# Rope queries relayed through memory by half batch, head and dimension: one store and four loads for a chunk instead of one and sixteen

## The chip, the cores and the metric

The kernel runs on one core of a Trainium2 chip. The metric is the device time of one execution in microseconds (us), the median of several runs. The core has four engines that compute (TensorE, VectorE, ScalarE and GpSimd; in the profile PE, DVE, ACT and POOL), 16 DMA engines that move data between memory (HBM) and on-chip memory (SBUF), and SyncE (SP), which here does nothing but wait for semaphores and issue DMAs, one after the other.

## The reference, cut to what matters

One decoder layer over 16 sequences of 128 tokens with 1024 features: latent attention with 32 heads, a cross attention, and a feed-forward part. The change touches the position-dependent half of the attention's scores:

```
q_rope = (c_q @ w_q_up_rope).reshape(b, s, H, DR).transpose(0, 2, 1, 3)      # H = 32 heads, DR = 64
q_rope = _apply_rope(q_rope, inv_freq, mscale)
scores = einsum('bhsr,btr->bhst', q_lat, c_kv) + einsum('bhsd,btd->bhst', q_rope, k_rope)
probs = softmax(where(causal, scores / sqrt(DN + DR), min))
```

After the attention come `x = x + out @ w_out`, then the cross attention and the feed-forward part, which the change leaves as they are.

## The kernel before

Everything is written out by hand: each engine has its own instruction list, and semaphores order them. The attention works through 16 passes ("quads" in the code, `m` from 0 to 15): two groups of 8 sequences, and for each group 8 quads of four heads. A pass has 8 steps (`s`), four for each of its two chunks (`c`) of 512 tokens, which are 4 sequences. Passes 0 to 6 are of the kind "full" (beside the attention they prepare the weights of the next quad), pass 7 is "switch" (tokens of the second group are loaded), passes 8 to 14 are "later" and 15 is "last", beside which the cross attention starts.

The rope queries of a chunk are computed for four heads at once. VectorE and GpSimd leave them in `rope_tmp`, `[128, 4, 512]`: the partition is head times 32 plus dimension, and the four slots are the first and the second half of the dimensions, each as a high and a low part, whose sum is the value. For the scores TensorE wants the four parts of one head pair on the partitions, in `qrope[c]`. Partitions can't be exchanged on chip in one step, so the data makes a round through memory: `relayout_out` stores `rope_tmp` to `parts_d[c]`, and `relayout_in` waits until that has landed and loads it back in the other order. There are 32 such rounds (16 passes, 2 chunks), of 1 MB each way. Both stand in SyncE's list, in front of whatever is issued next:

- in a full pass (`full_quad`) chunk 1's loads stand ahead of `load_raw_rope`, which brings the next quad's rope weights; ScalarE cuts them into high and low parts (L1924) in the middle of the same pass. Chunk 1's store stands ahead of a load of raw head weights (`load_head`, L678), which ScalarE reads at L1797 and L1798. Chunk 0's store and loads stand ahead of another `load_head`.
- in the switch pass (`switch_quad`) chunk 0's round stands ahead of `store_x1`, and chunk 1's ahead of `load_wqr(1)`, which brings the rope weights that TensorE needs in pass 8 (L55 on `at_wqr`).
- in pass 14 (`later_quad`) chunk 1's round stands ahead of `load_wvo` and, behind that, of the first rows `cr_x` of the cross attention (`load_x1`, L976), which VectorE reads in pass 15 at L2851, between two steps of the attention.
- at the start (`preparation`) chunk 0's round is on the way to the first scores (L1276).

DMAs issued by SyncE go through one queue and share the 16 DMA engines; TensorE waits for `qrope_in[c]` before the first step of each chunk.

Of the kernel before, what the change touches and what calls it, by code (L numbers as in the profile page):

```python
# [16 lines left out]
P = 128  # L17
# [5 lines left out]
HALF = DR // 2  # L23
# [24 lines left out]
def as_f32(ap):  # L48

    return ap.bitcast(F32)  # L50
# [9 lines left out]
def decoder(nc, a, scratch, out_d):  # L60
# [124 lines left out]
    with ctx:  # L185
# [22 lines left out]
        compressed = [home(4 * (PACK * c + KEYS), f"at_keys{c}", [P, CH]) for c in range(CPG)]  # L208
        wabs = [home(49152 + 6144 * i, f"at_wabs{i}", [P, 2, WABS_W], F32R) for i in range(2)]
        wqr = home(61440, "at_wqr", [P, 2, WQR_W], F32R)  # L210
        qrope0 = home(67584, "at_qrope0", [P, 2, HALVES, PAIR, HQ], F32R)
        qlat1 = home(83968, "at_qlat1", [P, HALVES, PAIR, HQ])
        rope_tmp = home(92160, "at_rope_tmp", [P, 4, CH])
        qlat0 = home(100352, "at_qlat0", [P, HALVES, PAIR, HQ])
# [17 lines left out]
        stage_at = (4 * (PACK + UNUSED), 4 * UNUSED, 198656)  # L232
        stage_0, stage_1, stage_2 = (home(o, f"at_stage{i}", [P, CH]) for i, o in enumerate(stage_at))
        stage = [[stage_0, stage_1], [stage_0, stage_2]]
        qrope1 = home(174080, "at_qrope1", [P, 2, HALVES, PAIR, HQ], F32R)
        ring = [home(200928 + 4 * ITEM_B * i, f"ab_raw{i}", [P, ITEM_B]) for i in range(2)]

        uv_hi = home(83456, "ab_uv_hi", [P, DV], F32R)
# [433 lines left out]
        def _(sp):  # L672
# [15 lines left out]

            def relayout_out(m, c):
                sp.wait_ge(rope_lo, 2 * (ROPES * m + c + 1))  # L690
                sp.dma_start(parts_d[c], rope_tmp[:]).then_inc(parts_out[c], 16)

            def relayout_in(m, c):
                sp.wait_ge(parts_out[c], 16 * (m + 1))
                of = parts_d[c].rearrange("(h p) j n -> j p h n", h=QUAD)
                for j in range(4):
                    for h in range(QUAD):
                        to = as_f32(qrope[c][j * HALF:(j + 1) * HALF, h // PAIR, :, h % PAIR])
                        sp.dma_start(to, of[SLOT_OF_PART[j]][:, h].rearrange("p (k q) -> p k q", q=HQ)).then_inc(  # L699
                            qrope_in[c], 16)  # L700

            def load_tokens(c, lo, hi, done):
                sp.dma_start(as_f32(tok[:, c, lo:hi]), tok_d[c][:, lo:hi]).then_inc(done[c], 16)
# [66 lines left out]
            def preparation():  # L770
                load_w_down(0)
                sp.dma_start(xt[:, 0, :], x_turned[ORDER[0]][:, 0, :]).then_inc(x_first_in, 16)
                load_w_down(1)
                sp.dma_start(xt[:, 1, :], x_turned[ORDER[0]][:, 1, :]).then_inc(xt_in[0], 16)
                load_w_down(2)
                load_turned(0, 1)
                load_w_down(3)
                load_w_down(4)
                load_turned(0, 2)
                load_x_tile(0, 0)  # L780
                load_w_down(5)
                load_x_tile(0, 1)
                load_turned(0, 3)
                load_x_tile(0, 2)
                sp.dma_start(ident[:], consts["ident"]).then_inc(ident_in, 16)
                load_x_tile(0, 3)
                load_w_turned(0)
                load_turned(1, 0)
                load_w_turned(1)
                load_turned(1, 1)  # L790
                for to, name in ((mask, "mask"), (cos, "cos"), (sin, "sin")):
                    sp.dma_start(to[:], consts[name]).then_inc(const_in, 16)
                for p in range(2):
                    sp.sem_inc(wabs_out[p], 16)
                    sp.sem_inc(wvo_out[p], 16 * len(RUNS[0]))
                sp.sem_inc(wqr_out, 16)

                def store_queries(i):
                    sp.wait_ge(tok_lo, 4 * i + QT)
                    sp.dma_start(tok_d[i][:, 0:KEYS], as_f32(tok[:, i, 0:KEYS])).then_inc(cq_out[i], 16)  # L800

                def store_keys(i):
                    sp.wait_ge(zeroed, 1)
                    sp.wait_ge(kr_lo, i + 1)
                    sp.wait_ge(tok_lo, 4 * i + 4)
                    sp.wait_ge(prep_turn_taken, lo_at["kv", i] + 1)
                    sp.dma_start(tok_d[i][:, KEYS:UNUSED], compressed[i][:]).then_inc(key_out[i], 16)
                    sp.dma_start(tok_d[i][:, KV_HI:PACK], as_f32(tok[:, i, KV_HI:PACK])).then_inc(key_out[i], 16)

                load_x_tile(1, 0)  # L810
                load_pair(0, 0, 0)
                load_x_tile(1, 1)
                load_pair(0, 1, 1)
                load_turned(1, 2)
                load_x_tile(1, 2)
                load_x_tile(1, 3)
                load_turned(1, 3)
                load_turned(2, 0)
                store_queries(0)
                load_turned(2, 1)  # L820
                for t in range(2):
                    load_x_tile(2, t)
                load_turned(2, 2)
                load_x_tile(2, 2)
                store_keys(0)
                load_x_tile(2, 3)
                sp.wait_ge(ab_mm, 2)
                load_head(0, 0, 0)
                store_wabs(0, 0, 2)
                load_turned(2, 3)  # L830
                sp.wait_ge(ab_mm, 4)
                load_head(0, 1, 1)
                store_wabs(0, 1, 4)
                load_turned(3, 0)
                store_queries(1)
                load_turned(3, 1)
                load_turned(3, 2)
                store_keys(1)


                sp.wait_ge(cq_out[1], 16)
                sp.wait_ge(key_out[1], 2 * 16)
                for t in range(BPC):
                    load_x_tile(3, t)
                load_raw_rope(0)
                sp.wait_ge(ab_mm, 6)
                load_head(0, 2, 0)
                load_turned(3, 3)
                sp.wait_ge(ab_mm, 8)
                load_head(0, 3, 1)  # L850
                store_wqr(0)
                relayout(0, 0)

                sp.wait_ge(qrope_in[0], 256)
                sp.wait_ge(prep_turn_taken, lo_at["x", KT * N - 1] + 1)
                load_x(0, 0)
                relayout_out(0, 1)
# [266 lines left out]
        def _(pe):  # L1124
# [136 lines left out]
            def score_ropes(m, s, group):  # L1261

                pair, c = place(s)
                if not (isinstance(m, int) and STEPS * m + s == 0):
                    pe.wait_ge(score_taken, STEPS * m + s)
                if s % UNITS == 0:
                    if group:
                        pe.wait_ge(key_in[c], 2 * 16)
                    pe.wait_ge(qrope_in[c], 256 * (m + s // STEPS + 1))
                if s == UNITS and not group:  # L1270

                    pe.wait_ge(kr_lo, N)
                    pe.wait_ge(tok_lo, 4 * N)
                rope_keys = tok[:, c, KR_HI:KR_HI + 2 * CH].rearrange("p (part t) -> p part t", part=2)
                for bl in range(2):
                    pe.matmul(score[:, bl], both_heads(qrope[c][:, pair, half_of(s, bl, 1)]), rope_keys[:, :, batch_cols(s, bl)],  # L1276
                              start=bl == 0, stop=False, skip_group_check=True)
                for bl in range(2):
                    pe.matmul(score[:, EARLY, :, early_keys(bl)], both_heads(qrope[c][:, pair, half_of(s, bl, 0)]),
                              rope_keys[:, :, early_cols(s, bl)], start=bl == 0, stop=False, skip_group_check=True)  # L1280

            def score_rests(m, s, taken):
# [1166 lines left out]
        def _(dve):  # L2449
# [287 lines left out]
            def opening():  # L2737
                first = USES_PREPARED
                largest(0, 0)
                dve.memset(as_f32(pT_both[HQ:P, :, :, 0:HQ]), 0.0)  # L2740
                query(N - 1, 1)
                query(N - 1, 2)
                recip(0, 0)

                latent(0, 1, 0, first + 4)
                latent(0, 1, 1, first + 5)
                largest(0, 1)
                turn(0, 0)
                dve.wait_ge(parts_out[0], 16)
                rope_keys(N - 1, (1,))  # L2750
                rope_half(0, 1, 0, first + 6)
                recip(0, 1)
                rope_half(0, 1, 1, first + 7)
                rope_keys(N - 1, (0,))
                direct_values(0, 0)
                value_sums(0, 0)
                kv_values(N - 1)

                dve.wait_ge(val_lo_done, 1)
                dve.wait_ge(prep_turn_taken, lo_at["kv", N - 1] + 1)  # L2760
                dve.sem_inc(added, 2)
                keys(N - 1)
# [367 lines left out]
def build(nc, a, out):  # L3130

    def scratch(name, shape):
# [1 line left out]

    decoder(nc, a, (scratch("tok_d", [CPG, P, PACK]), scratch("wabs_d", [QUADS, P, 2, 2 * PAIR * QL]),
                    scratch("wvo_d", [QUADS, P, 2, 2 * 7 * CH]), scratch("wqr_d", [QUADS, P, 2 * QT * 2 * P]),
                    scratch("parts_d", [CPG, P, 4, CH]), scratch("x1_d", [TOKENS // GROUPS, D]),
                    scratch("x2_d", [TOKENS, D]), scratch("ff_w_d", [7 * 3, P, 4 * CH])), out)


# [68 lines left out]
```

## Time and profile before

| | |
|---|---|
| median of 3 runs | 1919.39 us (1919.37 to 1921.03) |
| the profiled execution | 1921.1 us, of it 1919.3 us from the first to the last instruction (the span) |
| TensorE busy | 1899.9 us, 99% of the span |
| VectorE, ScalarE, GpSimd busy | 1546.6, 1183.9, 1039.1 us |
| mean clock granted to TensorE | 0.998 of full speed |
| DMA queue of SyncE | 207232 packets, 392.24 MB, 58.7% of the 16 engines' span |
| packets under 512 bytes | 146688 |

The span is what the instructions cover; the profiled execution is 1.8 us longer, for what lies before and after it. Busy shares are means over stages with different limits. A packet is what one DMA engine moves as one unbroken run.

### The profile page before, as it was taken

What the parts mean: (1) busy time and instruction counts of PE and PEld (TensorE: products, weight loads), DVE (VectorE), ACT (ScalarE), POOL (GpSimd) and SP (SyncE); (2) the same over time, 40 slices, a digit from 0 to 9 for tenths busy, and PEclk for the clock granted to TensorE, in tenths of its full rate; (3) what the DMA queues carried; (4) which work ended last, traced back from release to release, by engine and by line L of the source; (5) the groups of instructions that cost most, each with busy time, mean ns of one, the idle gap of its engine ahead of it and who ended that gap; (6) DMA issues with size and microseconds to landing.
All of it is one profiled execution on the core that took longest, in us unless ns stands there. A gap on an engine that the chain in (4) does not pass through costs nothing.

```text
span 1919.3 us, 32626 instructions
## 1 busy us (share of the span) xinstructions
PE 1899.9 (99%) x9920; PEld 1600.2 (83%) x9920; DVE 1546.6 (81%) x3168; ACT 1183.9 (62%) x2904; POOL 1039.1 (54%) x1019
## 2 busy tenths in 40 slices
PE   9999999999999999999999999999999999999999
PEld 7888888888888888888888888888887878888887
DVE  6778888887888888887888787887877889996677
ACT  5457767676758575765655556655655658766441
POOL 5468778787869696964655556555664511000000
PEclk9999999999999999999999999999999999999999
DMA  9838464646465655587646364464637287466644
GB/s 356 332 109 305 148 257 126 252 131 247 141 238 163 230 172 197 200 300 286 219 165 200 112 230 131 159 186 156 229 90 286 82 288 256 193 223 238 236 151 175
DMA packets 207323, 393.30 MB, mean 205 GB/s; under 512 B 146688, under 2 KB 147456, under 8 KB 188160
## 3 DMA queue, kind: packets, MB, share of 16 engines
q1 hardware_dynamic: 207232, 392.24, 58.7%
q8 instruction: 39, 0.64, 0.1%
q14 instruction: 52, 0.43, 0.1%
HBM read 236.46 MB, written 155.71 MB: 204 GB/s over the span
## 4 chain that ended last, share of the span: by engine, by line
PE 87%; DMA 5%; SPq 4%; DVE 2%; issue 1%; POOL 1%; ACT 0%; DVEq 0%; ACTq 0%; POOLq 0%
PE at_out L1325 9%; PE at_out L1329 9%; PE at_out L1326 9%; PE at_qbank L55 7%; PE at_qbank L57 7%; PE at_qbank L56 7%; SPq L699 3%; PE at_qbank L1649 3%; PE at_score L1649 3%; PE at_score L1286 2%; PE at_out L1649 2%; DMA parts_d<-at_rope_tmp 2%; PE at_score L1289 2%; PE at_turned L1300 2%; PE at_value L55 2%; PE at_value L56 2%
## 5 line engine op out<-in xcount | busy, mean ns | idle before, releaser
L2684 DVE TENSOR_TENSOR at_acc<-at_out,at_acc 128x512 f32<-128x512 f32 x640 | 438.8, 689 | 133.1 <-PE at_out L1329 127.0
L2315 POOL TENSOR_TENSOR at_acc<-at_stage,at_acc 128x512 f32<-128x512 f32 x256 | 331.7, 1296 | 175.6 <-ACT at_stage L1791 165.9
L1325 PE MATMUL at_out<-at_wvo,at_val_hi 128*128 128x512 f32 x896 | 365.5, 408 | 3.9 <-DVE at_acc L2684 3.0
L1329 PE MATMUL at_out<-at_wvo,at_val_lo 128*128 128x512 f32 x896 | 351.8, 393 | 0.0
L1326 PE MATMUL at_out<-at_wvo,at_val_hi 128*128 128x512 f32 x896 | 350.3, 391 | 0.0
L1791 ACT ACTIVATE at_stage<-at_out 128x512 f32<-128x512 f32 x256 | 152.4, 599 | 91.8 <-PE at_out L1329 80.1
L1329 PEld LDWEIGHTS at_out<-at_wvo,at_val_lo 128*128 128x128 f32 x896 | 168.4, 188 | 38.8
L1325 PEld LDWEIGHTS at_out<-at_wvo,at_val_hi 128*128 128x128 f32 x896 | 168.8, 188 | 32.9 <-DVE at_acc L2684 6.1
L1832 ACT ACTIVATE at_pT<-at_turned 128x256 fp32r<-128x256 f32 x128 | 48.9, 382 | 234.9 <-PE at_turned L1300 234.9
L1326 PEld LDWEIGHTS at_out<-at_wvo,at_val_hi 128*128 128x128 f32 x896 | 169.2, 189 | 26.1
L1827 ACT ACTIVATE at_probs<-at_probs,at_row_stats 128x128 f32<-128x128 f32 (+1 forms) x512 | 184.0, 361 | 8.4 <-DVE at_row_stats L2631 8.4
L2301 POOL TENSOR_TENSOR at_val_lo<-at_val_whole,at_val_hi 128x512 fp32r<-128x512 f32 x128 | 165.2, 1290 | 9.0 <-ACT at_val_hi L1845 8.3
L2274 POOL TENSOR_TENSOR at_probs<-at_probs,at_row_stats 128x256 f32<-128x256 f32 x128 | 78.7, 615 | 155.7 <-DVE at_row_stats L2636 155.2
L55 PE MATMUL at_qbank<-at_tok,at_wabs 128*128 128x512 f32 x384 | 153.1, 399 | 2.0 <-DVEq L2581 2.0
L57 PE MATMUL at_qbank<-at_tok,at_wabs 128*128 128x512 f32 x384 | 150.6, 392 | 0.0
L56 PE MATMUL at_qbank<-at_tok,at_wabs 128*128 128x512 f32 x384 | 149.3, 389 | 0.0
L2282 POOL TENSOR_TENSOR at_rope_tmp<-at_rope_tmp 128x512 f32<-128x512 f32 x62 | 79.0, 1295 | 81.1 <-DVE at_rope_tmp L2590 81.1
L2643 DVE TENSOR_TENSOR at_pT<-at_turned,at_pT 64x128 fp32r<-64x128 f32 x256 | 73.6, 288 | 48.6 <-ACT at_pT L1834 43.4
L1845 ACT ACTIVATE at_val_hi<-at_val_whole 128x512 fp32r<-128x512 f32 x128 | 80.7, 630 | 45.8 <-DVE at_val_whole L2664 45.7
L1812 ACT ACTIVATE at_qlat<-at_qbank 128x512 f32<-128x512 f32 x128 | 75.7, 591 | 47.3 <-PE at_qbank L57 47.3
L1827 ACT ACTIVATION_READ_ACCUMULATOR at_probs<-at_probs,at_row_stats 128x1 f32 x512 | 95.8, 187 | 0.0
L55 PEld LDWEIGHTS at_qbank<-at_tok,at_wabs 128*128 128x128 f32 x384 | 72.0, 187 | 23.7 <-DVEq L2581 8.2
(323 smaller groups left out, 5047.1 us busy)
## 6 DMA issues: line engine op xcount, KB each, us to landing
parts_d<-at_rope_tmp SPq DMA_DIRECT2D x32, 1024.0 KB, 6.5
at_qrope<-parts_d SPq DMA_DIRECT2D x512, 64.0 KB, 2.1
wvo_d<-at_wvo SPq DMA_DIRECT2D x16, 2048.0 KB, 8.2
at_wvo<-wvo_d SPq DMA_DIRECT2D x16, 2048.0 KB, 7.4
ff_w_d<-ff_w SPq DMA_DIRECT2D x21, 1024.0 KB, 6.3
ff_w<-ff_w_d SPq DMA_DIRECT2D x21, 1024.0 KB, 4.8
ab_raw<-in_w_heads SPq DMA_DIRECT2D x32, 576.0 KB, 5.0
wvo_d<-at_wvo SPq DMA_DIRECT2D x16, 1024.0 KB, 9.9
```

Source lines behind the costliest of these rows:

```text
L55: pe.matmul(out, w_hi, x_hi, start=first, stop=False)
L56: pe.matmul(out, w_hi, x_lo, start=False, stop=False)
L57: return pe.matmul(out, w_lo, x_hi, start=False, stop=last)
L1325: pe.matmul(out, hi, weight[:, 0], start=start, stop=False, skip_group_check=True)
L1326: pe.matmul(out, hi, weight[:, 1], start=False, stop=False, skip_group_check=True)
L1329: pe.matmul(out, lo, weight[:, 0], start=False, stop=True, skip_group_check=True).then_inc(out_ready, 1)
L1649: ins = pe.matmul(out, ff_w[i][:, k, cols], x[:, k, :], start=first, stop=last, skip_group_check=True)
L1791: act.activation(stage[group][z][:], outb[FACTORS[name][2]][:], ACT.Copy).then_inc(staged, 1)
L1827: ins = act.activation(rows, rows, ACT.Exp, bias=nmax[i][:, j:j + 1], accum_out=sums[i][:, j:j + 1])
L2301: pool.tensor_tensor(val_lo[s % 2][:, SUMS], val_whole[s % 2][:, SUMS], as_f32(val_hi[s % 2][:, high(SUMS)]), ALU.subtract).then_inc(val_s ...
L2315: pool.tensor_tensor(at, stage[group][z][:], at, ALU.add).then_inc(pool_added, 1)
L2684: dve.tensor_tensor(at, outb[FACTORS[name][2]][:], at, ALU.add).then_inc(added, 1)
```

## The change

The store writes `parts_d[c]` as `[32, 128, 64]`: first the slot and the half batch (4 slots times 8 halves of 64 tokens), then head and dimension, then the 64 tokens. Each unbroken run in memory is then 64 numbers, 256 bytes, where it was 2048 numbers, 8 KB. In that order the load of one slot is a single DMA over 32 partitions, with 32 runs of 256 bytes for each; there are four loads where there were sixteen (one for each slot and head). `qrope` has its dimensions in another order, `[half, head, token]` instead of `[head pair, half, head of the pair, token]`; the 128 numbers that TensorE loads at once lie together in both. The waits on `qrope_in` count to 64 instead of 256. Apart from that one `memset` of VectorE's opening is placed three instructions later.

```
-        qrope0 = home(67584, "at_qrope0", [P, 2, HALVES, PAIR, HQ], F32R)
+        qrope0 = home(67584, "at_qrope0", [P, HALVES, QUAD, HQ], F32R)
...
             def relayout_out(m, c):
                 sp.wait_ge(rope_lo, 2 * (ROPES * m + c + 1))
-                sp.dma_start(parts_d[c], rope_tmp[:]).then_inc(parts_out[c], 16)
+                sp.dma_start(parts_d[c].rearrange("n p q -> p n q"),
+                             rope_tmp[:].rearrange("p j (k q) -> p (j k) q", q=HQ)).then_inc(parts_out[c], 16)
 
             def relayout_in(m, c):
                 sp.wait_ge(parts_out[c], 16 * (m + 1))
-                of = parts_d[c].rearrange("(h p) j n -> j p h n", h=QUAD)
+                of = parts_d[c].rearrange("(j k) (h p) q -> j p (k h) q", j=4, h=QUAD)
                 for j in range(4):
-                    for h in range(QUAD):
-                        to = as_f32(qrope[c][j * HALF:(j + 1) * HALF, h // PAIR, :, h % PAIR])
-                        sp.dma_start(to, of[SLOT_OF_PART[j]][:, h].rearrange("p (k q) -> p k q", q=HQ)).then_inc(
-                            qrope_in[c], 16)
+                    to = as_f32(qrope[c][j * HALF:(j + 1) * HALF]).rearrange("p k h q -> p (k h) q")
+                    sp.dma_start(to, of[SLOT_OF_PART[j]]).then_inc(qrope_in[c], 16)
...
-                sp.wait_ge(qrope_in[0], 256)
+                sp.wait_ge(qrope_in[0], 64)
...
-                    pe.wait_ge(qrope_in[c], 256 * (m + s // STEPS + 1))
+                    pe.wait_ge(qrope_in[c], 64 * (m + s // STEPS + 1))
...
-                    pe.matmul(score[:, bl], both_heads(qrope[c][:, pair, half_of(s, bl, 1)]), rope_keys[:, :, batch_cols(s, bl)],
+                    pe.matmul(score[:, bl], both_heads(qrope[c][:, half_of(s, bl, 1), heads]), rope_keys[:, :, batch_cols(s, bl)],
...
-                dve.memset(as_f32(pT_both[HQ:P, :, :, 0:HQ]), 0.0)
                 query(N - 1, 1)
                 query(N - 1, 2)
                 recip(0, 0)
+                dve.memset(as_f32(pT_both[HQ:P, :, :, 0:HQ]), 0.0)
...
-                    scratch("parts_d", [CPG, P, 4, CH]), scratch("x1_d", [TOKENS // GROUPS, D]),
+                    scratch("parts_d", [CPG, 4 * CH // (SEQ // 2), P, SEQ // 2]), scratch("x1_d", [TOKENS // GROUPS, D]),
```

From the change on, line numbers above 694 are one lower.

The order of instructions changes on SyncE alone, apart from the memset. This is the start of a full pass in SyncE's list, the loads of chunk 1 (`at_qrope_92`) between a load of raw weights and `load_raw_rope`, before:

```order
L674 DMA ab_raw_93<-in_w_heads 128x2x512
L694 REGISTER_ALU
L699 DMA at_qrope_92<-parts_d 32x8x64 x16
L681 ISA
L681 DMA at_rope_tmp<-in_w_rope 128x768
```

And with the change:

```order
L674 DMA ab_raw_93<-in_w_heads 128x2x512
L695 REGISTER_ALU
L699 DMA at_qrope_92<-parts_d 32x32x64 x4
L681 ISA
L681 DMA at_rope_tmp<-in_w_rope 128x768
```

Twelve DMAs fewer stand ahead of the raw rope weights; the neighbours are the same.

The second place is the switch pass, from chunk 0's store to the load of the rope weights of pass 8 (`at_wqr`), in SyncE's list before:

```order
L691 DMA parts_d<-at_rope_tmp 128x2048
L699 DMA at_qrope_61<-parts_d 32x8x64 x16
L716 DMA x_d<-at_acc 128x4x1024
L706 DMA at_keys_57<-tok_d 128x512
...
L713 DMA at_acc<-in_x 128x2x1024
L691 DMA parts_d<-at_rope_tmp 128x2048
L699 DMA at_qrope_92<-parts_d 32x8x64 x16
L747 DMA at_wqr<-wqr_d 128x1536
L743 DMA at_wvo_68<-wvo_d 128x4096
```

And with the change:

```order
L691 DMA parts_d<-at_rope_tmp 128x32x64
L699 DMA at_qrope_61<-parts_d 32x32x64 x4
L715 DMA x_d<-at_acc 128x4x1024
L705 DMA at_keys_57<-tok_d 128x512
...
L712 DMA at_acc<-in_x 128x2x1024
L691 DMA parts_d<-at_rope_tmp 128x32x64
L699 DMA at_qrope_92<-parts_d 32x32x64 x4
L746 DMA at_wqr<-wqr_d 128x1536
L742 DMA at_wvo_68<-wvo_d 128x4096
```

Nothing changes places; each store has 32 runs of 64 numbers for each partition instead of one of 2048, and 12 loads fewer follow it.

## Rows read from the trace of the kernel before

**Rows 1.** The page: busy us of each engine (share of the span) xinstructions

```profile
PE 1899.9 (99%) x9920; PEld 1600.2 (83%) x9920; DVE 1546.6 (81%) x3168; ACT 1183.9 (62%) x2904; POOL 1039.1 (54%) x1019
```

**Rows 2.** Waits of PE, 150 to 720 us: us in total, times, longest

```profile
PE at_value L55 <- DVE at_pT L2643: 4.0, 6, 1.0
```

**Rows 3.** Timeline, SyncE, a full pass: start us, us, issue, count

```profile
236.11 7.95 SPq L699 DMA_DIRECT2D at_qrope<-parts_d  x16
```

**Rows 4.** Timeline, ACT and PE, the same pass: [idle before <-releaser]

```profile
247.76 0.85 ACT L1924 ACTIVATE at_wqr<-at_rope_tmp 128x768 fp32r<-128x768 f32 x1 [1.07 <-DMA at_rope_tmp<-in_w_rope]
250.15 0.38 PE L55 MATMUL at_value<-at_pT,at_tok 128*128 128x256 f32 x1 [1.05 <-DVE at_pT L2643]
```

**Rows 5.** Timeline, SyncE, the switch pass

```profile
842.31 9.24 SPq L699 DMA_DIRECT2D at_qrope<-parts_d  x16
...
861.80 0.47 SPq L691 DMA_DIRECT2D parts_d<-at_rope_tmp  x1
880.55 9.30 SPq L699 DMA_DIRECT2D at_qrope<-parts_d  x16
889.89 0.45 SPq L747 DMA_DIRECT2D at_wqr<-wqr_d  x1
```

**Rows 6.** Timeline, PE, start of pass 8

```profile
894.58 0.79 PE L55 MATMUL at_qbank<-at_tok,at_wqr 128*128 128x512 f32 x1 [2.91 <-DMA at_wqr<-wqr_d]
```

**Rows 7.** Windows: us, busy of each engine, PEclk (granted clock), DMA share, GB/s

```profile
250.20:253.60 3.40, 3.10 (x15) 2.39 (x16) 3.14 (x7) 2.64 (x6) 2.84 (x3) 1.00 1.01 432
894.30:897.70 3.40, 3.12 (x7) 2.48 (x8) 0.00 (x0) 0.00 (x0) 0.00 (x0) 0.50 1.00 429
1474.60:1478.00 3.40, 3.40 (x13) 2.90 (x12) 2.12 (x4) 0.15 (x1) 1.97 (x3) 0.50 1.02 419
```

**Rows 8.** Timeline, SyncE, from pass 14 into pass 15

```profile
1450.61 7.73 SPq L699 DMA_DIRECT2D at_qrope<-parts_d  x16
1458.60 1.42 SPq L743 DMA_DIRECT2D at_wvo<-wvo_d  x3
1460.36 1.01 SPq L976 DMA_DIRECT2D cr_x<-x_d  x2
```

**Rows 9.** Timeline, DVE and PE, pass 15

```profile
1471.47 0.69 DVE L2851 BATCH_NORM_STATS2 cr_stats<-cr_x 128x6 f32<-128x512 f32 x1 [2.87 <-DMA cr_x<-x_d]
1474.26 0.54 PE L1325 MATMUL at_out<-at_wvo,at_val_hi 128*128 128x512 f32 x1 [3.05 <-DVE at_acc L2684]
```

**Rows 10.** DMA queues, 331.2 to 333 us: packets, MB, share of 16 engines

```profile
q1 hardware_dynamic: 1562, 0.44, 110.4%
```

**Rows 11.** The same of 113.5 to 117.3 us

```profile
q1 hardware_dynamic: 144, 1.05, 66.1%
```

**Rows 12.** The same of 1916.5 to 1918.6 us

```profile
q1 hardware_dynamic: 303, 0.27, 37.0%
```

**Rows 13.** The page, DMA issues: count, KB each, median us to landing

```profile
at_qrope<-parts_d SPq DMA_DIRECT2D x512, 64.0 KB, 2.1
```

**Rows 14.** Timeline of SyncE and ACT just behind chunk 1's store, full pass

```profile
320.47 0.34 SPq L678 DMA_DIRECT2D ab_raw<-in_w_heads  x1
...
329.60 0.30 ACT L1797 ACTIVATE ab_uv_hi<-ab_raw 128x128 fp32r<-128x128 f32 x1
```

**Rows 15.** DMA issues, 319.8 to 320.6 us: KB each, us to landing

```profile
ab_raw<-in_w_heads SPq DMA_DIRECT2D x1, 576.0 KB, 5.5
```

**Rows 16.** Timeline, SyncE and PE, the first round

```profile
117.32 7.98 SPq L699 DMA_DIRECT2D at_qrope<-parts_d  x16
126.88 0.40 SPq L709 DMA_DIRECT2D at_acc<-in_x  x1
...
127.82 0.40 PE L1276 MATMUL at_score<-at_tok,at_qrope 128*128 128x256 f32 x2
```

**Rows 17.** Timeline, DVE, the opening

```profile
131.54 0.48 DVE L2740 MEMSET at_pT<- 64x512 f32 x1 [0.16 <-issue]
...
134.78 0.43 DVE L2620 TENSOR_TENSOR at_probs<-at_score,at_mask 128x256 f32<-128x256 f32 x1 [1.36 <-PE at_score L1289]
```

More of the change, by code:

```diff
@@ L234, in decoder @@
         stage = [[stage_0, stage_1], [stage_0, stage_2]]
-        qrope1 = home(174080, "at_qrope1", [P, 2, HALVES, PAIR, HQ], F32R)
+        qrope1 = home(174080, "at_qrope1", [P, HALVES, QUAD, HQ], F32R)
         ring = [home(200928 + 4 * ITEM_B * i, f"ab_raw{i}", [P, ITEM_B]) for i in range(2)]
@@ L1273, in score_ropes @@
                     pe.wait_ge(tok_lo, 4 * N)
+                heads = slice(pair * PAIR, (pair + 1) * PAIR)
                 rope_keys = tok[:, c, KR_HI:KR_HI + 2 * CH].rearrange("p (part t) -> p part t", part=2)
                 for bl in range(2):
-                    pe.matmul(score[:, bl], both_heads(qrope[c][:, pair, half_of(s, bl, 1)]), rope_keys[:, :, batch_cols(s, bl)],
+                    pe.matmul(score[:, bl], both_heads(qrope[c][:, half_of(s, bl, 1), heads]), rope_keys[:, :, batch_cols(s, bl)],
                               start=bl == 0, stop=False, skip_group_check=True)
                 for bl in range(2):
-                    pe.matmul(score[:, EARLY, :, early_keys(bl)], both_heads(qrope[c][:, pair, half_of(s, bl, 0)]),
+                    pe.matmul(score[:, EARLY, :, early_keys(bl)], both_heads(qrope[c][:, half_of(s, bl, 0), heads]),
                               rope_keys[:, :, early_cols(s, bl)], start=bl == 0, stop=False, skip_group_check=True)
```

## Prediction

> **What bounds the kernel now.** I read the page first: TensorE is busy for 1899.9 of 1919.3 us [rows 1]. A change that takes nothing from TensorE can win only part of the 19.4 us left, so the question is which of TensorE's gaps a round of rope queries stands behind. I then took its waits (who released it), looked at the timeline just before each, and followed the releaser back. None of the waits names `qrope` itself, but three kinds go back to SyncE's list, where the round keeps something else from being issued.
>
> First, the full passes. TensorE waits six times for the transposed probabilities, 4.0 us in all [rows 2]. In the pass shown it idles 1.05 us at 250.15; ScalarE, which turns the probabilities ahead of that, had itself idled 1.07 us for the raw rope weights [rows 4]. These are issued right behind sixteen loads, which took SyncE 7.95 us from 236.11 on, and landed at 247.76 [rows 3, 4].
>
> Second, the switch pass. TensorE idles 2.91 us for `at_wqr` until 894.58 [rows 6]. That load was issued at 889.89, behind 9.30 us of sixteen loads, which began when the store issued at 861.80 had landed, at 880.55 [rows 5]. Right behind the stall the granted clock is 0.50 (1.2 GHz, the lower level) for 3.40 us or so [rows 7]; work done in that time at half speed costs 1.7 us more.
>
> Third, pass 15. VectorE idles 2.87 us for `cr_x` until 1471.47, and TensorE then 3.05 us for VectorE [rows 9]. `cr_x` was issued at 1460.36 behind 3.5 MB of `at_wvo`, issued at 1458.60, and that behind 7.73 us of sixteen loads [rows 8]. Again the clock is 0.50 for 3.40 us [rows 7], 1.7 us more. Behind the 1.05 us stall in the full pass it stays 1.00, 2.4 GHz [rows 7].
>
> So 4.0 + (2.91 + 1.7) + (3.05 + 1.7) = 13.4 us is the most that the change can win.
>
> **The price of small packets.** Each load has always moved packets of 256 bytes: 4096 for a round. In a stretch with the queue full of them the 16 engines were 110.4% busy with 1562 packets in 1.8 us [rows 10]: by time, 1.8 x 16 / 1562 = 18.4 ns each. A round's loads are 256 packets for each DMA engine, 4.7 us; now they take 7.7 to 9.3 us because SyncE issues sixteen. Four issues don't bound them (one takes 0.5 us, from 7.73 / 16), so I take 2.1 us from issue to landing for 64 KB [rows 13], less its own 0.3 us of packets (16 x 18.4 ns), plus 4.7: 6.5 us from the first issue to the last landing. Now it is 126.88 - 117.32 = 9.6 us in the first round [rows 16].
>
> The store is the disputed cost. Today its 1 MB runs in 8 KB packets: 66.1% of 3.8 us x 16 engines for the megabyte [rows 11], 2.5 us of a full queue. With the change it is 256 packets for each engine too. No row shows 256-byte packets written to memory. From below it can't be less than today's 2.5 us. The nearest row with small packets into memory is the output's end, mostly 1 KB packets: 37.0% of 2.1 us x 16 over 303 packets is 41 ns each [rows 12]; 1 KB at the pace of the 8 KB packets would be 39 ns, so a write carries no visible extra. From above I take twice the 18.4 ns. I use 18.4 ns, as the loads show: 4.7 us, 2.2 us more than now for each of the 32 stores.
>
> A rule of the Trainium skill speaks against this: the page "DMA: Bandwidth & Descriptors", section Specifications, asks for at least 512 B for line rate, below which the DMA engine does a read-modify-write. For the loads' 256 bytes the trace shows no more than 18.4 ns, 223 GB/s; for writes to memory nothing here shows it. By that rule, if it doubled the write, the sum would be that of the first rival below, where it is worked out from rows.
>
> **The sum.**
> - Full passes: the loads start at 236.11 as before and have landed by 242.6 (6.5 us), some 1 us later where a raw-weight load is ahead. The raw rope weights, 0.4 MB right behind them, land about 3 us earlier than 247.76; ScalarE was free at 246.69 (247.76 - 1.07). The wait goes, six times: -4.0.
> - Switch pass: chunk 0's last load is issued 0.5 us before 842.31 + 9.24 and lands 2.1 later, 853.2. With the change the store lands 2.2 later and the loads 6.5 after: 851.0, 2.2 earlier. From there to 880.55 the queue is full of what stands behind (the store issued at 861.80 needs 18.7 us), so chunk 1's store lands 2.2 earlier and 2.2 later: 880.55 again. Four loads (1.8 + 4.7) and 768 KB at 0.4 MB/us (rows 7 has 429 GB/s), 1.9 us: `at_wqr` is there at 889.0; TensorE wants it at 891.67. The wait and its dip go: -4.6. Margin 2.7 us.
> - Pass 15: the store lands at 1452.8, the loads at 1459.3 instead of about 1460.0 (1458.34, less 0.5, plus 2.1). `at_wvo` is issued in time and starts right behind them, about 0.8 us earlier than now, and so does `cr_x`. TensorE's stall falls from 3.05 to 2.2. Whether the clock then stays up is open: it does after 1.05 us and not after 2.91. I take it that it does: -0.8 - 1.7 = -2.5.
> - First round: landed at 117.32 + 2.2 + 6.5 = 126.0 instead of 126.9, and TensorE wants it at 127.82 [rows 16]: 0.
> - Raw head weights behind chunk 1's store: now issued at 320.47, landed 5.5 later at 326.0, read at 329.60 [rows 14, 15]. 3.6 us of cover, of which 2.2 go: 0.
> - The memset: 0.48 us, moved into VectorE's 1.36 us of idle time before 134.78 [rows 17]: 0. Without that cover it would be 0.5 us.
> - TensorE's own work: the same matmuls on 128 neighbouring numbers, 0.
>
> Together -11.1 us. The profiled execution took 1921.1 us, 1.7 above the median of the runs; against the median, **1919.4 - 11.1 = 1908.3 us**.
>
> **Rivals.**
>
> *The stores are slow (slower).* One mechanism: a 256-byte packet into memory takes much longer than 18.4 ns. It decides at about 26 ns. At twice, 36.8 ns, a store is 9.4 us, 6.9 more than now. The raw head weights land 6.9 later against 3.6 of cover, ScalarE waits 3.3 us in each of seven passes, at most 23.1 us; the first scores wait 2.9 + 1.7; `at_wqr` lands 3.8 later than now; pass 15 loses 4.0; the 4.0 of the full passes are still won: +31.5, 1951 us. At 26 ns (4.15 more): +3.9, +0.2, -1.6, +1.3, -4.0, about 0: 1919. For it: nothing shows such writes. Against it: rows 12. Chance 0.16 for above, 0.07 for around 26 ns (no change), 0.10 for 21 to 25 ns (1911 to 1916).
>
> *Four big loads take as long as sixteen small ones (slower).* They read memory in runs of 256 bytes 8 KB apart, where they now read 2 KB together. If they take 7.7 us or more, nothing is won in full passes, `at_wqr` comes 4.4 later (two stores), pass 15 loses 2.2 and the first round 1.3: +7.9, 1927 us. It decides from 7 us of packets on. Against it: when the queue was full the engines kept their pace [rows 10]. Chance 0.05.
>
> *The clock dips in pass 15 all the same:* -9.4, 1910 us. *Or the whole stall there goes,* if the loads run a little faster: -13.4, 1906 us. Both belong to the forecast's own range, 1905.5 to 1911; chance of all this 0.57.
>
> **How the numbers follow.** What a measurement here can tell from no change is 0.2%, 3.8 us. Faster: 0.57 + 0.10 + 0.05 of other partial gains = 0.72. Same: 0.07. Slower: 0.16 + 0.05 = 0.21, the two slow rivals. The range runs from 1904.5 (all gains, a little more) into the slow cases, which lie between 1921 and 1951: at 1926 about 0.15 are left above.
>
> **What the profile would show.** Right: 1 MB stores landing some 2 us later than now where the queue is empty (4.7 to about 7), four issues in 2 to 5 us; no ScalarE wait at L1924 and no gap at L55 `at_value` in full passes; no stall around 890; one dip of the clock or none. Wrong: packets of the store above 26 ns, ScalarE idle at L1797, TensorE idle at L1276.

## The result, and the profile after

The changed kernel takes **1907.59 us** (median of 4 runs, 1906.41 to 1910.56), the kernel before 1919.76 (median of 4 runs beside them, 1919.37 to 1921.03). The ratio is 0.9942, 95% interval 0.9926 to 0.9957: 12.2 us less. The profiled execution took 1908.6 us, with a span of 1906.8. Forecast were 1908.3 and a range of 1904.5 to 1926.

The page of the changed kernel, busy time of each engine, the packets and the issues of the round:

```profile
PE 1895.3 (99%) x9920; PEld 1597.3 (84%) x9920; DVE 1545.4 (81%) x3168; ACT 1183.8 (62%) x2904; POOL 1039.5 (55%) x1019
...
DMA packets 328154, 393.27 MB, mean 206 GB/s; under 512 B 271616, under 2 KB 272384, under 8 KB 313088
...
parts_d<-at_rope_tmp SPq DMA_DIRECT2D x32, 1024.0 KB, 7.1
at_qrope<-parts_d SPq DMA_DIRECT2D x128, 256.0 KB, 4.6
```

TensorE's busy time fell by 4.6 us against [rows 1] with the same 9920 matmuls; two stretches of 3.4 us at half the clock [rows 7] that are gone make 3.3 of these by an estimate (half of the 3.12 and 3.40 us of work in them). The rest of the gain, 7.9 of the 12.5 us by which the span is shorter, is idle time. The longest of TensorE's waits from 150 to 720 us, in us in total, times and longest:

```profile
PE at_qbank L55 <- DVEq L2581: 2.0, 7, 0.3
```

The wait for `at_pT` of [rows 2] is no longer there. (The line numbers of the two kernels agree again at L1276 and up to L2740, since the change adds a line there too, `heads = slice(pair * PAIR, (pair + 1) * PAIR)`.) The timeline of SyncE in the changed kernel in the first round, in a full pass, in the switch pass and in pass 14, at the places of [rows 16, 3, 5, 8]:

```profile
113.14 0.38 SPq L691 DMA_DIRECT2D parts_d<-at_rope_tmp  x1
118.68 2.73 SPq L699 DMA_DIRECT2D at_qrope<-parts_d  x4
125.36 0.40 SPq L708 DMA_DIRECT2D at_acc<-in_x  x1
...
236.28 4.95 SPq L699 DMA_DIRECT2D at_qrope<-parts_d  x4
241.42 0.86 SPq L681 DMA_DIRECT2D at_rope_tmp<-in_w_rope  x1
...
854.48 0.47 SPq L691 DMA_DIRECT2D parts_d<-at_rope_tmp  x1
873.54 2.62 SPq L699 DMA_DIRECT2D at_qrope<-parts_d  x4
876.21 1.08 SPq L746 DMA_DIRECT2D at_wqr<-wqr_d  x1
...
1442.17 2.75 SPq L699 DMA_DIRECT2D at_qrope<-parts_d  x4
1445.19 1.93 SPq L742 DMA_DIRECT2D at_wvo<-wvo_d  x3
```

The first store of the kernel before:

```profile
112.82 0.33 SPq L691 DMA_DIRECT2D parts_d<-at_rope_tmp  x1
```

Three spans matter here. The first store takes 118.68 - 113.14 = 5.5 us until the loads can be issued, where it took 117.32 - 112.82 = 4.5 (its loads are in [rows 16]). The first round's loads take 125.36 - 118.68 = 6.7 us against 9.6 [rows 16]. And in the full pass the raw weights are issued 5.1 us behind the first load, where they stood behind 8 us of issues [rows 3]. What the other engines show, as timelines of ScalarE, VectorE and TensorE:

```profile
246.75 0.83 ACT L1924 ACTIVATE at_wqr<-at_rope_tmp 128x768 fp32r<-128x768 f32 x1
...
886.72 0.39 PE L55 MATMUL at_qbank<-at_tok,at_wqr 128*128 128x512 f32 x1
...
1461.26 0.69 DVE L2851 BATCH_NORM_STATS2 cr_stats<-cr_x 128x6 f32<-128x512 f32 x1 [2.20 <-DMA cr_x<-x_d]
...
1464.05 0.50 PE L1325 MATMUL at_out<-at_wvo,at_val_hi 128*128 128x512 f32 x1 [2.38 <-DVE at_acc L2684]
```

Neither L1924 nor `at_wqr` has a wait behind it now [rows 4, 6]; of the large stalls only that for `cr_x` is left, 2.38 us instead of 3.05 [rows 9]. The granted clock stays at 1.00 behind it (windows):

```profile
1464.10:1467.50 3.40, 3.40 (x22) 2.95 (x23) 2.92 (x6) 1.25 (x4) 2.23 (x3) 1.00 1.02 411
```

To place gains and losses, the table gives, for each profiled execution, the start of TensorE's first L1276 of a pass (the last row but one is the last of the 8 steps of pass 15): for before in us, for the others as the difference to it. e1 to e4 are the experiments below.

| | before | changed | e1 small store | e2 weights first | e3 big loads | e4 double store |
|---|---|---|---|---|---|---|
| pass 0 | 127.82 | +0.29 | +1.24 | +0.05 | +0.07 | +0.34 |
| pass 1 | 213.63 | +0.17 | +1.22 | +0.04 | -0.05 | +0.76 |
| pass 7 | 767.49 | -4.77 | +2.20 | -5.06 | -5.10 | -0.11 |
| pass 8 | 854.47 | -4.79 | +2.71 | -5.04 | -5.11 | +4.96 |
| pass 9 | 941.39 | -9.47 | +4.78 | -8.23 | -9.79 | +1.20 |
| pass 15 | 1435.37 | -9.54 | +9.16 | -7.67 | -9.88 | +8.57 |
| its last step | 1504.81 | -11.67 | +10.92 | -8.02 | -14.29 | +10.05 |
| end | 1919.31 | -12.48 | +11.22 | -8.48 | -14.44 | +10.04 |

So the full passes 1 to 6 gave 4.9 us, pass 8 (with the stall of [rows 6]) 4.7, pass 15 2.1, and the part behind it 0.8.

### The profile page after: what moved, and what is told of

Same layout as the page of the kernel before. It is cut to its first block, busy times and chain, and to the rows that moved or that the text cites. A ratio compares the mean times of both kernels' runs of the same rounds, so it can differ in the third digit from the quotient of the medians.

```text
span 1906.8 us, 32242 instructions
## 1 busy us (share of the span) xinstructions
PE 1895.3 (99%) x9920; PEld 1597.3 (84%) x9920; DVE 1545.4 (81%) x3168; ACT 1183.8 (62%) x2904; POOL 1039.5 (55%) x1019
## 4 chain that ended last, share of the span: by engine, by line
PE 89%; POOL 3%; DVE 2%; DMA 2%; issue 1%; SPq 1%; ACT 1%; DVEq 0%; POOLq 0%; ACTq 0%
PE at_out L1325 10%; PE at_out L1329 9%; PE at_out L1326 9%; PE at_qbank L55 7%; PE at_qbank L57 7%; PE at_qbank L56 7%; PE at_qbank L1649 3%; PE at_score L1649 3%; PE at_score L1286 3%; PE at_out L1649 2%; PE at_score L1289 2%; PE at_turned L1300 2%; PE at_value L55 2%; PE at_value L56 2%; PE at_value L57 2%; PE at_value L1649 2%
## 5 line engine op out<-in xcount | busy, mean ns | idle before, releaser
L55 PE MATMUL at_qbank<-at_tok,at_wabs 128*128 128x512 f32 x384 | 153.0, 398 | 2.0 <-DVEq L2581 2.0
L55 PEld LDWEIGHTS at_qbank<-at_tok,at_wabs 128*128 128x128 f32 x384 | 72.0, 187 | 23.6 <-DVEq L2581 8.1
```

Of the source, the lines that this page charges most:

```text
L55: pe.matmul(out, w_hi, x_hi, start=first, stop=False)
```

## The experiments

My theory: a round's loads used to keep other loads from being issued, and the gain is theirs; the small-packet store costs a little and hides. The rivals: the gain has to do with fewer issues as such, or the store's price is far from what I took, or the loads' time has another cause than their packets.

**The store with sixteen loads (e1).** The changed layout and store, with sixteen loads. These read the new layout, in runs of 256 bytes where they read 2 KB together, so that it isn't the store alone that differs from the kernel before:

```
-                sp.dma_start(parts_d[c], rope_tmp[:]).then_inc(parts_out[c], 16)
+                sp.dma_start(parts_d[c].rearrange("n p q -> p n q"),
+                             rope_tmp[:].rearrange("p j (k q) -> p (j k) q", q=HQ)).then_inc(parts_out[c], 16)
...
-                of = parts_d[c].rearrange("(h p) j n -> j p h n", h=QUAD)
+                of = parts_d[c].rearrange("(j k) (h p) q -> j h p k q", j=4, h=QUAD)
...
-                        sp.dma_start(to, of[SLOT_OF_PART[j]][:, h].rearrange("p (k q) -> p k q", q=HQ)).then_inc(
+                        sp.dma_start(to, of[SLOT_OF_PART[j]][h]).then_inc(
```

> The kernel before with the change's memory layout and its store in runs of 256 bytes, but still sixteen loads for a round. If the store costs what the first round of the changed kernel showed (5.5 us from issue to landing against 4.5 before, 1.0 more): the rope weights of pass 8 land 2.0 later (two stores), TensorE's wait for them grows from 2.9 to about 5; pass 15 loses 1.0, the first round 0.2; the raw head weights keep their cover: +3.3 us, 1923. If it costs the 2.2 us of the forecast: 4.4 in the switch pass, 2.2 in pass 15, 1.3 in the first round, +7.9 us, 1928. If, against both, writing in small runs were what gains time: below 1918.

Measured: 1930.63 us (5 runs), ratio 1.0055 (1.0042 to 1.0068), **slower** by 10.8 us, more than either theory gave (3.3 and 7.9). Timelines of SyncE and TensorE, and TensorE's waits from 940 to 1436 us:

```profile
113.18 0.38 SPq L691 DMA_DIRECT2D parts_d<-at_rope_tmp  x1
118.70 8.35 SPq L700 DMA_DIRECT2D at_qrope<-parts_d  x16
```
```profile
899.24 0.74 PE L55 MATMUL at_qbank<-at_tok,at_wqr 128*128 128x512 f32 x1 [4.79 <-DMA at_wqr<-wqr_d]
...
1484.07 0.79 PE L1326 MATMUL at_out<-at_wvo,at_val_hi 128*128 128x512 f32 x1 [3.70 <-DVE at_acc L2685]
```
```profile
PE at_qbank L55 <- DMA at_wqr<-wqr_d: 2.7, 6, 0.6
```

and its window behind the stall of 3.70 us:

```profile
1484.00:1491.00 7.00, 6.93 (x26) 6.17 (x27) 5.03 (x14) 1.55 (x6) 3.04 (x5) 0.58 1.04 408
```

The store costs 118.70 - 113.18 = 5.5 us again. The sixteen loads take about as long as before: from first issue to last landing the median of the rounds for passes 9 to 15 is 9.6 us, in the kernel before 9.4. So the reading in another order costs little, and most of the loss is the store's. `at_wqr` in pass 8 fits the price of 1 us (4.79 instead of 2.91, expected about 5). Three other places do not. The first scores begin 1.24 us later, where 0.2 was expected by this price. Passes 1 to 7 lose 1.5. Pass 15 loses 1.8 instead of 1.0: the stall is only 0.65 longer, but the clock is low for about 6 us behind it, where it was for 3.4 [rows 7]. What both theories lacked altogether is in the row before the window: two stores, 1 us later each, make TensorE wait for `at_wqr` in all six passes from 9 to 14. In the kernel before it landed there only 0.1 to 1.2 us before TensorE took it (in pass 10 at 1060.53, read at 1060.67). The table has 4.4 us for these passes, of which the wait names 2.7. So the store is not free: in front of sixteen loads it costs the kernel 11 us, and it is the four loads that turn this into a gain of 12.

**The order alone (e2).** The kernel before, old store and sixteen loads, two weight loads moved ahead of them:

```
-                relayout_in(q, 1)
                 if not (isinstance(q, int) and q == 0):
+                    sp.wait_ge(parts_out[1], 16 * (q + 1))
                     load_raw_rope(q + 1)
+                relayout_in(q, 1)
...
-                relayout(m + 1, 1)
+                relayout_out(m + 1, 1)
                 sp.wait_ge(rope_mm, 2 * ROPES * (m + 2))
                 load_wqr(1)
+                relayout_in(m + 1, 1)
```

> The kernel before, with the 8 KB store and the sixteen loads, but with two loads of weights moved ahead of the sixteen: the raw rope weights in full passes and at_wqr in the switch pass. If the gain of the change comes from what these loads waited behind: the full passes win 4 to 5 us, the switch pass 4.6 with its dip of the clock, pass 15 nothing: 1919.8 - 9 = 1910.5, and the wait for cr_x stays at about 2.9. If the gain comes from fewer issues or fewer descriptors as such, or if the queries are then late in their turn (sixteen loads behind 0.4 MB more): less than half of that, 1915 or more, with waits of TensorE at L1276.

Measured: 1912.11 us (5 runs), ratio 0.9955 (0.9942 to 0.9969), **faster** by 7.7. Timeline of SyncE in e2, the full pass and the switch pass, then TensorE:

```profile
236.28 0.34 SPq L681 DMA_DIRECT2D at_rope_tmp<-in_w_rope  x1
236.67 8.00 SPq L699 DMA_DIRECT2D at_qrope<-parts_d  x16
...
857.32 0.43 SPq L747 DMA_DIRECT2D at_wqr<-wqr_d  x1
876.20 8.42 SPq L699 DMA_DIRECT2D at_qrope<-parts_d  x16
```
```profile
897.75 0.49 PE L1327 MATMUL at_out<-at_wvo,at_val_hi 128*128 128x512 f32 x1 [0.89 <-DMA at_wvo<-wvo_d]
...
1466.09 0.50 PE L1327 MATMUL at_out<-at_wvo,at_val_hi 128*128 128x512 f32 x1 [2.55 <-DVE at_acc L2686]
```

With all sixteen loads still there the full passes win 5.1 us, as in the change (4.9), and neither shows the wait for `at_pT` of [rows 2]. So their gain needs neither fewer loads nor the new layout, only that the raw weights are issued earlier. The switch pass gives 3.2 instead of 4.7: `at_wvo`, still behind the sixteen loads, is now late by 0.89. Pass 15 stays at a stall of 2.55. The theory holds for two of the three places; in the third this run moved nothing.

**Large packets for the loads (e3).** The store does the whole rearrangement, one store for each head, and the loads read 8 KB in one piece:

```
+                for h in range(QUAD):
+                    sp.dma_start(parts_d[c][:, :, h],
+                                 rope_tmp[h * HALF:(h + 1) * HALF].rearrange("p j (k q) -> p (j k) q", q=HQ)).then_inc(
+                        parts_out[c], 16)
...
+                of = parts_d[c].rearrange("p (j k) h q -> j p (k h q)", j=4)
```

> The changed kernel with the rearrangement done by the store alone: four stores in runs of 256 bytes (one for each head), and four loads that read 8 KB in one piece. If small packets are what bounds a round's loads (6.7 us from first issue to last landing): they fall to about 4, four store issues cost about 1.2, and the wait for cr_x in pass 15 shrinks by 2 to 3 us: 1905.5. If four issues and their latency bound them, or the four stores take longer than one: nothing or a loss, 1907.5 to 1911.

Measured: 1906.83 us (5 runs), ratio 0.9933 (0.992 to 0.9946), which the intervals do not tell from the change's 0.9942. The time lies between those of the two theories, but the loads did not fall to the 4 us of the first. The page of e3:

```profile
DMA packets 202714, 393.28 MB, mean 206 GB/s; under 512 B 142080, under 2 KB 142848, under 8 KB 183552
...
at_qrope<-parts_d SPq DMA_DIRECT2D x128, 256.0 KB, 4.9
```

It moves 38% fewer packets, yet a load takes 4.9 us instead of 4.6. My account of the loads, 256 packets of 18.4 ns for each engine, gave the right 6.5 us for what looks like the wrong reason; e6 tests it the other way round. That pass 15 has no stall for `cr_x` in this execution (the table's -14.29) says little, as e5 and e10 will show: the same list without this edit had 2.38, 1.16 and none.

**What bounds a round's loads (e6, e9).** Both write the same megabyte with four loads that each fill all 128 partitions instead of 32. They leave the rearrangement out, so that the scores are computed from other numbers, and they also read memory in another order than the runs they stand beside. e6 keeps packets of 256 bytes:

```
-                of = parts_d[c].rearrange("(j k) (h p) q -> j p (k h) q", j=4, h=QUAD)
+                of = parts_d[c].rearrange("n p q -> p n q")
...
+                    some = slice(HALVES * j, HALVES * (j + 1))
+                    sp.dma_start(to[:, some], of[:, some]).then_inc(qrope_in[c], 16)
```

> The changed kernel with four loads of the same size, the same packets of 256 bytes and the same places in the list, but each writes to all 128 partitions (8 of the 32 runs of each) and not to 32; this leaves the rearrangement out, so the scores are of other numbers. If the loads are bound by writing to 32 partitions at a time (the 8 KB packets of the big loads took 6.8 us for a round too): a round's loads fall from 6.7 us to about 5.6, the 3.6 us of a full queue that a store of 256-byte packets takes plus 2, and the wait in pass 15 shrinks by about 1: 1906.5. If they are bound by the number of packets, as the forecast had it: 6.7 us as before, 1907.6.

e9 does it on e3, in runs of 2 KB (`some = slice(CH * j, CH * (j + 1))`).

> As the whole-width loads, with the same part left out, but by four loads of 2 KB runs (and the four stores by head, as with the big loads): 512 packets on all 128 partitions, where the big loads had 128 packets on 32 at a time. If the 32 partitions are the bound: some 4.5 us from first issue to last landing against 6.8 of the big loads. If not: 6.8 again.

Measured: e6 1906.86 us (5 runs), ratio 0.9943 (0.993 to 0.9957); e9 1906.11 (one run). Take the loads of chunk 1 in pass 14: SyncE issues the first of the four at 1442.17 in the changed kernel, 1441.45 in e3, 1441.66 in e6 and 1441.38 in e9, and the last at 1443.98, 1442.76, 1443.49 and 1442.70. The DMA issues of that last one, KB and us to landing, in the changed kernel:

```profile
at_qrope<-parts_d SPq DMA_DIRECT2D x1, 256.0 KB, 4.8
```

in e3:

```profile
at_qrope<-parts_d SPq DMA_DIRECT2D x1, 256.0 KB, 5.6
```

in e6:

```profile
at_qrope<-parts_d SPq DMA_DIRECT2D x1, 256.0 KB, 3.8
```

and in e9:

```profile
at_qrope<-parts_d SPq DMA_DIRECT2D x1, 256.0 KB, 4.4
```

From the first issue to the last landing a round takes (1443.98 + 4.8 - 1442.17 = 6.6, the others likewise):

| | packets of 256 bytes | larger packets |
|---|---|---|
| 32 partitions at a time | 6.6 us (changed) | 6.9 us (e3, 8 KB) |
| all 128 partitions | 5.6 us (e6) | 5.7 us (e9, 2 KB) |

This is one round of 32. Over the 14 rounds that bring the queries of passes 9 to 15 the medians are 6.6, 6.8, 5.8 and 5.7 us (changed, e3, e6, e9), which says the same: the size of the packets makes little difference in either line, and the loads on all partitions are 0.8 to 1.2 us faster. For chunk 0 of passes 1 to 7 they are 6.65, 6.85, 6.0 and 6.8: there the 2 KB packets on all partitions gain nothing (for pass 3 e9 issues the first load at 380.40 and the last at 381.73, and this lands 5.3 us later). So e6, with the same packets, shows that their number is not what held the loads at 6.6 us, and the width is a part of it but not the whole. The 4.5 us that was expected of e9 came in no round. The Trainium skill (SBUF — State Buffer, "Door 1: The DMA port swizzle") says that 32 neighbouring partitions reach only 8 of SBUF's 16 ports, at 27.2 GB/s each. An estimate from that page is 1.05 MB / 218 GB/s = 4.8 us for a round, nearly the figure that my packets gave (4.7), and the direction of the table agrees with it. Its size does not: by this estimate twice the ports would save 2.4 us, and 1.0 to 1.2 were saved. What holds the wide loads at 5.6 us, and why e9 is no faster in these rounds for passes 1 to 7, stays open.

**The store's price doubled (e4).** Each store issued twice, the first to other memory, and every wait for `parts_out` doubled:

```
+                sp.dma_start(parts_d[CPG + c].rearrange("n p q -> p n q"),
+                             rope_tmp[:].rearrange("p j (k q) -> p (j k) q", q=HQ)).then_inc(parts_out[c], 16)
                 sp.dma_start(parts_d[c].rearrange("n p q -> p n q"),
```

> The changed kernel with every store done twice, the first time to other memory, so that the cost of small packets into memory is paid twice more where it stands on a path. If such a store takes 3.6 us of a full queue (as its first one shows in the changed kernel): first round +0.8, rope weights of pass 8 7.2 later against 4.5 of margin, 2.7, pass 15 +3.6, up to 0.8 in each of seven passes for the raw head weights, 1.7 for each dip of the clock that returns: 1918 to 1924. If it takes 4.7, as forecast: 1.9 + 4.9 + 4.7 + 13 + two dips of 1.7, 1935. If stores ran beside the other transfers: below 1912.

Measured: 1931.31 us (6 runs), ratio 1.0055 (1.0042 to 1.0068): 23.7 more than the change. SyncE in e4, first round:

```profile
112.48 0.38 SPq L691 DMA_DIRECT2D parts_d<-at_rope_tmp  x1
...
121.67 0.33 SPq L701 DMA_DIRECT2D at_qrope<-parts_d  x1
```

121.67 - 112.48 = 9.2 us for two, 5.5 for one: the second costs 3.7, so the price is the 3.6 of the expectation and not 4.7. The sum, 1918 to 1924, was still too low by 7 us. Waits in e4 of ScalarE and VectorE (150 to 1430 us) and TensorE (940 to 1436):

```profile
ACT ab_uv_hi L1799 <- DMA ab_raw<-in_w_heads: 7.2, 7, 1.3
```
```profile
DVE at_rope_tmp L2592 <- DMA parts_d<-at_rope_tmp: 15.5, 8, 3.3
```
```profile
PE at_qbank L55 <- DMA at_wqr<-wqr_d: 4.6, 4, 2.8
```

The first I had in the sum (up to 0.8 each; it is 1.0 of ScalarE, while TensorE's own waits behind it are 0.2 to 0.7). The second I had not: VectorE must not write the next `rope_tmp` before the store has read it, and behind such a wait TensorE idles for `at_pT`, with a dip of the clock behind. Timeline of VectorE and TensorE:

```profile
848.14 0.69 DVE L2592 TENSOR_TENSOR at_rope_tmp<-at_qbank,at_cos 128x512 f32<-128x512 f32 x1 [3.25 <-DMA parts_d<-at_rope_tmp]
...
851.50 0.38 PE L55 MATMUL at_value<-at_pT,at_tok 128*128 128x256 f32 x1 [2.27 <-DVE at_pT L2645]
```

The third is `at_wqr` in passes 9 to 14 again, up to 2.78 us at 1231.98, with another dip. In pass 8, where I had expected 2.7 us for it, the table has only 0.9 (10.67 - 9.75). Of the 22.5 us between the two profiled executions 0.6 lie in pass 0, 4.1 in passes 1 to 6 (4.66 at pass 7, less 0.59 at pass 1), 5.1 in pass 7, 8.4 in passes 8 to 14 (18.11 - 9.75), 3.6 in pass 15 and 0.8 behind it. No run has four loads behind a store of 8 KB packets, so what a single small-packet store costs the changed kernel as a whole isn't shown; a second one costs it 23.7 us.

**The last stall (e5, e7, e8).** e5 is the changed kernel again, timed beside the next two. e7 issues the first row of `cr_x` in pass 14 ahead of `at_wvo`; e8 is that on top of e3.

```
                 relayout(m + 1, 1)
+                if before_last:
+                    sp.wait_ge(rope_mm, 2 * ROPES * (LAST + 1))
+                    load_x1(0)
                 sp.wait_ge(out_ready, outs_later(m, 8))
                 load_wvo(q1, 1)
```

> The changed kernel as it is, once more, to be timed beside the others of this group. Expected by every theory: 1907.6 us within 1.5, with one stall of TensorE above 0.6 us, that of 2.4 in pass 15.

> The changed kernel with the load of the first cr_x row moved in pass 14 to right behind the queries' loads, ahead of 3.5 MB of at_wvo. If the wait in pass 15 is nothing but this row behind at_wvo: it goes, 2.4 us of TensorE, 1905.2. If at_wvo, 1.2 us later by it, is what TensorE wants next, the wait only changes its name: 1906.5 to 1908.

> The early row together with the four stores and the 8 KB loads. Both take away the same wait, the last one above 0.6 us in pass 15, so together they should give no more than one of them: 1904.9 to 1906.8. If the big loads helped elsewhere too (their median is 0.8 below that of the changed kernel, their profiled run 2.0): 1903.5 or less.

Measured, 5 runs each: e5 1907.16 (0.9938, 0.9924 to 0.9951), e7 1907.17 (0.9939, 0.9926 to 0.9953), e8 1906.87 (0.9938, 0.9924 to 0.9951). Nothing to tell between them. TensorE in e5:

```profile
1462.45 0.50 PE L1325 MATMUL at_out<-at_wvo,at_val_hi 128*128 128x512 f32 x1 [1.16 <-DVE at_acc L2684]
```

and in e7:

```profile
1531.69 0.33 PE L1548 MATMUL at_score<-at_ident,cr_probs 128*128 128x128 f32 x1 [1.14 <-ACT cr_probs L2017]
...
1779.89 0.50 PE L1651 MATMUL at_qbank<-ff_hi,ff_w 128*128 128x512 f32 x1 [0.75 <-DMA ff_w<-ff_w_d]
```

The early row does take the wait in pass 15 away: e7's trace has none for VectorE there. But the wait was only 1.16 us in e5, the unchanged list, not 2.38, and e7 gives back what it won: 1.14 us in the cross attention, behind a wait of VectorE for a later row of `cr_x`, and 0.75 where feed-forward weights arrive (e5 has waits of 0.29 and 0.61 at the same two places). The expected 2.4 us rested on one execution of a wait that varies by more than a microsecond.

**The memset put back (e10).**

```
+                dve.memset(as_f32(pT_both[HQ:P, :, :, 0:HQ]), 0.0)
                 query(N - 1, 1)
                 query(N - 1, 2)
                 recip(0, 0)
-                dve.memset(as_f32(pT_both[HQ:P, :, :, 0:HQ]), 0.0)
```

> The changed kernel with the memset at its old place, ahead of two queries of the preparation. If moving it was worth nothing, TensorE's work of pass 1 begins where it does in the changed kernel, within 0.3 us, and the memset's 0.48 us lie in idle time of VectorE at either place. If it held something up: 0.5 us in the opening.

Measured: 1907.53 us (one run, the kernel before beside it 1916.83); pass 1 begins at 213.93 against 213.80 in the changed kernel and 213.45 in e5. VectorE in e10, and in the changed kernel:

```profile
131.82 0.48 DVE L2740 MEMSET at_pT<- 64x512 f32 x1 [0.16 <-issue]
...
135.06 0.42 DVE L2620 TENSOR_TENSOR at_probs<-at_score,at_mask 128x256 f32<-128x256 f32 x1 [1.36 <-PE at_score L1289]
```
```profile
133.62 0.48 DVE L2743 MEMSET at_pT<- 64x512 f32 x1 [0.16 <-issue]
...
135.07 0.42 DVE L2620 TENSOR_TENSOR at_probs<-at_score,at_mask 128x256 f32<-128x256 f32 x1 [0.97 <-PE at_score L1289]
```

The step behind it starts at 135.06 and 135.07. Moving it was worth nothing that shows here. In this execution the stall for `cr_x` in pass 15 is missing (TensorE has no gap above 0.2 us from 1420 to 1500 us): with 2.38 and 1.16 it is the third value from the same list of that pass.

## Why the prediction was right, by its own steps

- **Full passes, -4.0:** 4.9 measured. Right in mechanism: e2 alone reproduces it. The 0.9 more seems to be of the same cause, since e2, with nothing else changed in these passes, has 5.1; the view of waits names only 4.0. It was closer than I had it: in the pass shown the raw rope weights landed at 246.01, 1.7 us earlier than before and not 3, and ScalarE took them at 246.75.
- **Switch pass, -4.6:** 4.7 measured. `at_wqr` was forecast 8.45 us behind the store's landing (889.0 - 880.55); it landed at 882.2, 8.7 behind 873.5, and TensorE reads it at 886.72. The margin was 4.5 us, not 2.7: pass 8 began 4.8 us earlier than before, but chunk 1's store landed 7.0 earlier (873.54 against 880.55), so 2.2 us sooner within the pass than I had it.
- **Pass 15, -2.5:** 2.1 by its last step and 2.9 by the end in the profiled execution; the stall forecast at 2.2 was 2.38, and the clock did not dip, as I took it. Other executions of the same list had 1.16 and none, and pass 15 gained 3.3 and 4.4 by its last step there (e5, e10). So the size was partly luck, and so is a part of the total.
- **First round, memset, TensorE's own work, 0:** right for the first two. The loads landed at 125.36 (forecast 126.0) and the first scores began 0.29 later than before, without a wait for them; e10 shows the memset. TensorE's busy time fell by 1.3 us more than the two dips explain, and no run takes this apart.
- **The store, +2.2:** mis-sized, too dear. In the changed kernel, DMA queue of 114.5 to 117.5 us, packets, MB and share:

```profile
q1 hardware_dynamic: 3364, 0.86, 126.0%
```

  3.0 x 16 / 3364 = 14.3 ns for a packet of 256 bytes written to memory, not 18.4, so 3.7 us for a megabyte, which e4 confirms; from issue to landing the store costs 1.0 more in the first round, not 2.2, and mostly 0.5 to 1.3 more in the rounds for passes 2 to 7. My 18.4 came from loads on 32 partitions at a time [rows 10].
- **The loads, 6.5 us:** right size (6.6 to 6.7), wrong cause, as e3 and e6 show: that the size agrees is luck. For larger packets the forecast would have promised a gain that isn't there (e3), and for the same packets on all partitions it would have missed one of 1.0 us in the loads (e6). Right behind a load of raw weights a round takes more, 8.1 to 9.3 us in passes 1 to 6, where I had allowed for about 7.5. What this did to the raw rope weights stands under the full passes.
- **The rule against it** (the Trainium skill, DMA: Bandwidth & Descriptors, Specifications: below 512 B a read-modify-write): in the changed kernel 14.3 ns is 286 GB/s of 256-byte writes, 1.0 us more for a store where the queue is free. So they are slower than the 8 KB packets, as the page has it, but a doubled write does not show.
- **Rival "four loads as slow as sixteen", 1927:** e1, with loads that take as long as before, is near that case, and takes 1930.6. The step that failed there is my list of places: I had left out the small margin of `at_wqr` in passes 9 to 14, 4.4 us. The rival "the stores are slow" lacked that too, and VectorE's wait for the store.

## What to carry to other kernels

When a queue is issued in order, price a group of transfers by what stands behind it, in every pass and not only where something already waits: the same store costs 11 us in front of sixteen loads, and in front of four the whole change gains 12. Before rows of packets are turned into a price, ask what else the transfers have in common, here the 32 partitions that they write. Two explanations gave nearly the same microseconds, and only runs that changed the one and left the other told them apart; even so they left a part of the time unexplained. And a stall of two microseconds seen in one execution should be seen in a second before work goes into it.

## What the runs showed of the hardware that was not expected

- In a full queue packets of 256 bytes cost the same to and from memory when all 128 partitions take part: 14.3 ns in the full queue for the store, and 1.5 x 16 / 1678 = 14.3 for the loads of e6. The loads on 32 partitions take 1.5 x 16 / 1434 = 16.7. The DMA queue of e6 and then of the changed kernel from 1445 to 1446.5 us:

```profile
q1 hardware_dynamic: 1678, 0.44, 130.4%
```
```profile
q1 hardware_dynamic: 1434, 0.36, 120.6%
```

- The length of a stall alone does not say whether the clock falls behind it. It stayed at 1.00 behind 2.38 us in the changed kernel and fell to 0.50 behind 2.27 us in e4, where the row of its windows is:

```profile
852.64:856.00 3.36, 3.36 (x10) 2.59 (x9) 2.74 (x8) 2.63 (x11) 3.10 (x3) 0.50 1.12 351
```

  What TensorE did just ahead does not tell them apart either: in the 5.5 us that end with the stall it was busy for 3.24 us in e4 and for 3.12 in the changed kernel (the second figure of each row). Why the clock fell in the one and not in the other stays open. The windows in e4 and then in the changed kernel:

```profile
846.00:851.50 5.50, 3.24 (x22) 2.59 (x20) 3.32 (x8) 2.01 (x5) 0.80 (x1) 1.00 0.85 187
```
```profile
1458.55:1464.05 5.50, 3.12 (x15) 2.25 (x13) 3.23 (x8) 2.23 (x11) 1.17 (x1) 1.00 1.03 388
```

  A dip costs about half of its 3.4 us, by an estimate from the matmuls in it: those of 128x512 take 0.63 to 0.79 us each in e1 (L55 at 899.24) and 0.39 at the full clock (at 886.72).
